# Edge sums of a graph layer: the node one-hot held still, the edge rows moved through it and accumulated by block

## The reference

```python
scores = jnp.einsum('ehd,ehd->eh', q[dst], k[src]) * scale      # 8 heads of 32
m = jax.ops.segment_max(scores, dst, num_segments=n)
ex = jnp.exp(scores - m[dst])
z = jax.ops.segment_sum(ex, dst, num_segments=n)
attn = ex / z[dst]
agg = jax.ops.segment_sum(attn[:, :, None] * v[src], dst, num_segments=n)
```

## Time and profile before

| | us |
|---|---|
| median of 3 runs | 5668.79 |
| the profiled execution, its span | 5667.8 |
| plan, clearing and first node pass | 0 to 576 |
| edge pass, layer 0 | 576 to 1972 |
| merge of ends | 1972 to 2117 |
| node pass "middle" | 2117 to 2905 |
| edge pass, layer 1 | 2907 to 4498 |
| merge of ends | 4498 to 4646 |
| node pass "last" | 4646 to 5560 |
| selection and store | 5560 to 5668 |

### The profile page before, as it was taken

The page is one execution under the profiler, slowest core; times in us unless marked ns, Lnnn a source line. Parts: engine busy times, 40 slices in busy tenths (PEclk is TensorE's granted clock), DMA queues, the critical chain, the costliest instruction groups (busy, mean ns, idle before and its releaser), DMA issues. The chain is left out here.

```text
span 5667.8 us, 110095 instructions
## 1 busy us (share of the span) xinstructions
PE 4558.0 (80%) x23706; PEld 3347.3 (59%) x23707; DVE 3879.3 (68%) x10653; ACT 1667.3 (29%) x5501; POOL 1786.4 (32%) x1733
## 2 busy tenths in 40 slices
PE   1666899999999857888878888888888658999993
PEld 1333566666666536666655555555555438888882
DVE  5888777777777756666666666666666746666665
ACT  0111233333333302222223222332332204444440
POOL 1000566666666400000035555555555300000000
PEclk9777999999999958999989998998998859999995
DMA  1111666666666401111135555555555310000001
GB/s 52 57 56 54 181 185 184 183 186 182 185 186 185 139 13 51 45 42 42 42 111 162 161 161 154 160 168 153 159 167 153 108 41 23 22 22 22 22 19 45
DMA packets 370226, 607.17 MB, mean 107 GB/s; under 512 B 136374, under 2 KB 221174, under 8 KB 370006
## 3 DMA queue, kind: packets, MB, share of 16 engines
q0 software_dynamic: 136960, 447.68, 27.1%
q1 hardware_dynamic: 233078, 157.70, 9.7%
HBM read 557.69 MB, written 48.27 MB: 107 GB/s over the span
## 5 line engine op out<-in xcount | busy, mean ns | idle before, releaser
L608 POOL DMA_INDIRECT edge_kv<-kv,edge_idx x1664 | 1742.0, 1047 | 2444.0 <-DMA edge_idx<-step_src 1248.1
L772 PE MATMUL edge_sums<-edge_sel,edge_kv 128*128 128x130 f32 x6656 | 1195.7, 304 | 126.4 <-DVE edge_kv L699 120.3
L815 ACT COPY acc<-edge_sums 128x384 f32 x1664 | 798.9, 480 | 1515.7 <-PE edge_sums L774 1478.8
L772 PEld LDWEIGHTS edge_sums<-edge_sel,edge_kv 128*128 128x128 f32 x6656 | 944.0, 198 | 448.8 <-issue 376.9
L734 PE MATMUL edge_q<-qc,edge_spread 128*128 x3328 | 939.7, 406 | 99.9 <-DVE edge_kv L650 76.1
L650 DVE TENSOR_TENSOR edge_kv<-edge_kv,edge_q 128x512 f32<-128x512 f32 x832 | 561.0, 674 | 447.7 <-DMA edge_kv<-kv,edge_idx 357.1
L734 PEld LDWEIGHTS edge_q<-qc,edge_spread 128*128 128x128 f32 x3328 | 583.4, 195 | 260.6 <-issue 213.5
L774 PE MATMUL edge_sums<-edge_sel,edge_wm 128*40 128x130 f32 x3328 | 713.7, 297 | 0.0
L699 DVE TENSOR_TENSOR edge_kv<-edge_kv,edge_wm 128x512 f32<-128x512 f32 x832 | 568.1, 683 | 113.5 <-ACT edge_wm L803 113.5
L657 DVE TENSOR_REDUCE edge_score<-edge_kv 128x16 f32<-128x512 f32 x832 | 557.8, 670 | 0.2
L774 PEld LDWEIGHTS edge_sums<-edge_sel,edge_wm 128*40 128x40 f32 x3328 | 256.8, 117 | 214.2 <-issue 22.6
(11 more groups left out here) (370 smaller groups left out, 5498.6 us busy)
## 6 DMA issues: line engine op xcount, KB each, us to landing
edge_rel<-step_rel SPq DMA_DIRECT2D x208, 256.0 KB
edge_kv<-kv,edge_idx POOLq DMA_INDIRECT x1664, 3.7
edge_flags<-step_flags SPq DMA_DIRECT2D x416, 32.0 KB
kv<-first_kv_out SPq DMA_DIRECT2D x49, 256.0 KB
kv<-middle_kv_out SPq DMA_DIRECT2D x49, 256.0 KB
h<-first_h SPq DMA_DIRECT2D x49, 128.0 KB
middle_h_in<-h SPq DMA_DIRECT2D x49, 128.0 KB
middle_v_in<-kv SPq DMA_DIRECT2D x49, 128.0 KB
```

The source lines that it names most:

```text
L608: nc.gpsimd.indirect_dma_start(kv[:, lane, j, :], None, dram["kv"], bass.IndirectOffsetOnAxis(ap=idx[:, turn[0], j:j + 1], axis=0)).then_i ...
L772: t.matmul(out[:, half * SELW:(half + 1) * SELW], kv[:, lane, j, D + half * P:D + (half + 1) * P], one_hot, start=True, stop=True)
L815: act_p.tick(s.copy(acc[:, :, bass.ds(at, P)], out[:, :, 0:P]), turn, f"acc{j}")
```

## The change

The product of a step is turned round. The one-hot of the node in its block (`sel`, now 128 columns, relative to the block and not to the step's first node) is the stationary side, and the edge's row of 272 columns (256 values, 8 weights, 8 maxima) is moved through it, so that sums arrive with nodes on the partitions. Steps of one block accumulate in one of four PSUM banks; a two-column matmul of zeros clears the accumulation state of the bank of the next block. ScalarE copies after every step the bank of the block before to `acc`, which now has 272 columns a block. The two end nodes are no columns of the one-hot any more: after each half of a group (four steps) four small matmuls with 2 stationary columns each write them at partitions 0, 32, 64 and 96 of a further bank, from where ScalarE copies them and SyncE stores them to memory. The gathers of steps 0 to 3 wait for `ends0`, of steps 4 to 7 for `ends1`. Register values are loaded for a pair at a time: two for q and four for the banks on TensorE, four on ScalarE. `qc` is now just q, `merge_ends` adds into `acc`, and neither is cleared.

```diff
-SELW = P + 2
-ZM = 40
+ROW = KV + 2 * H
+SUMS = 4
+BANKED = 512
+HALF = G // 2
...
+def values_of(nc, engine, ap, most):
+    engines = [e for e in mybir.ALL_ENGINES if e.name == engine]
+    assert len(engines) == 1
+    return nc.values_load_multi_w_load_instructions(ap, engines, min_val=0, max_val=most)[1]
...
-        kv = sb("kv", [P, 2, G, KV])
+        kv = sb("kv", [P, 2, G, ROW])
...
-        psa = [ps(f"sums{i}", [P, 512]) for i in range(ABUFS)]
+        psa = ps("sums", [P, SUMS * BANKED])
+        pse = ps("end_sums", [P, 512])
...
+            def store_ends(turn):
+                lane = turn[0]
+                act_p.wait(sp, turn, "ends1", beside=s_clear)
+                into = dram["erows"].rearrange("(b q w) n -> w b q n", q=HALF, w=2)
+                for q in range(HALF):
+                    sp.dma_start(into[:, bass.ds(number(later(turn, -1), 2), 4), q, :],
+                                 ends[32 * q:32 * q + 2, lane // 2, :, :]).then_inc(s_ends[lane // 2], 16)
...
                     if not first:
-                        pe_p.wait(pool, later(turn, -2), f"sums{j}", beside=s_clear)
+                        pe_p.wait(pool, later(turn, -2), f"ends{j // HALF}", beside=s_clear)
...
+            def sums_at(turn, m):
+                return values_of(nc, "PE", regs_s[0:1, turn[0], 4 * m:4 * m + 4], (SUMS - 1) * BANKED)
...
                 elif what == "tail":
+                    place = sums_at(turn, m)
                     dve_p.wait(pe, turn, f"value{m}")
                     for j in (2 * m, 2 * m + 1):
-                        if j >= ABUFS:
-                            act_p.wait(pe, turn, f"ends{j - ABUFS}")
+                        if j >= 2:
+                            act_p.wait(pe, turn, f"acc{j - 2}")
                         elif not earliest:
-                            act_p.wait(pe, later(turn, -1), f"ends{j + G - ABUFS}")
-                        one_hot = sel[:, j, :]
-                        out = psa[j % ABUFS]
-                        for half in range(2):
-                            t.matmul(out[:, half * SELW:(half + 1) * SELW],
-                                     kv[:, lane, j, D + half * P:D + (half + 1) * P], one_hot, start=True, stop=True)
-                        pe_p.tick(t.matmul(out[0:ZM, 2 * SELW:3 * SELW], wm[:, lane, j, :], one_hot,
-                                           start=True, stop=True), turn, f"sums{j}")
+                            act_p.wait(pe, later(turn, -1), f"acc{j + G - 2}")
+                        here, ahead = place[2 * (j % 2)], place[2 * (j % 2) + 1]
+                        t.matmul(psa[:, bass.ds(ahead, 2)], zeros[:, :], zeros[:, 0:2], start=True, stop=True,
+                                 skip_group_check=True)
+                        pe_p.tick(t.matmul(psa[:, bass.ds(here, QC)], sel[:, j, :], kv[:, lane, j, D:ROW],
+                                           start=False, stop=True, skip_group_check=True), turn, f"sums{j}")
+                    if m % 2 == 1:
+                        half = m // 2
+                        if half:
+                            act_p.wait(pe, turn, "ends0")
+                        elif not earliest:
+                            act_p.wait(pe, later(turn, -1), "ends1")
+                        for q in range(HALF):
+                            j = half * HALF + q
+                            mm = t.matmul(pse[32 * q:32 * q + 2, 0:QC], tab[:, turn[0], j, 2:4], kv[:, lane, j, D:ROW],
+                                          start=True, stop=True)
+                        pe_p.tick(mm, turn, f"ends{half}")
...
-                        out = psa[j % ABUFS][:, 0:3 * SELW].rearrange("p (c n) -> p c n", c=3)
-                        act_p.tick(s.copy(acc[:, :, bass.ds(at, P)], out[:, :, 0:P]), turn, f"acc{j}")
-                        act_p.tick(s.copy(ends[:, :, bass.ds(number(turn, 2 * G) + 2 * j, 2)], out[:, :, P:SELW]),
-                                   turn, f"ends{j}")
+                        act_p.tick(s.copy(acc[:, bass.ds(at, QC)], psa[:, bass.ds(bank, QC)]), turn, f"acc{j}")
+                    if m % 2 == 1:
+                        half = m // 2
+                        pe_p.wait(act, turn, f"ends{half}")
+                        if turn[0] % 2 == 0 and half == 0:
+                            room_for_ends(turn)
+                        act_p.tick(s.copy(ends[:, turn[0] // 2, 2 * lane + half, :], pse[:, 0:QC]),
+                                   turn, f"ends{half}")
```

In `plan_steps` six passes over 896 elements for the columns go, and the tables are written as one (`tab`: column, last, two end flags) with three register tables. In `merge_ends` the end rows are loaded from memory in three cuts, and 13 rounds of turning and scaling become three. In the node passes the stage `sums_t` (two transposes, a copy) and the addition of `qc` go:

```diff
-                elif stage == "sums_t":
-                    if exists(later(turn, -2)):
-                        pe_p.wait(act, later(turn, -2), "acc_t")
-                    act_p.tick(s.copy(ab[:, i, :, :], acc[:, 0:2, bass.ds(number(turn, P), P)]), turn, "acc")
...
-def clear_sums(nc, keep):
-
-    with nc.Block() as block:
-        @block.vector
-        def _(dve):
-            nc.vector.memset(keep["acc"][:, :, :], 0.0)
```

More of the change, by code:

```diff
@@ L185, in plan_steps @@
         col = sb("col", [P, SC, P])
[L186 removed]
+        both = sb("both", [P, SC, P])
         nf = sb("nf", [P, SC, P])
@@ L489, in edge_pass @@
         s_table = [sem(f"table{i}") for i in range(4)]
+        s_ends = [sem(f"ends{i}") for i in range(2)]
         s_row = [[sem(f"rows{i}_{j}") for j in range(G)] for i in range(2)]
@@ L501, in edge_pass @@
         dve_p.begin(dve_steps)
-        pe_p.begin([f"q{m}" for m in range(PAIRS)] + ["score_t", "max_t"] + [f"sums{j}" for j in range(G)])
-        act_p.begin(["weights"] + [f"{n}{j}" for j in range(G) for n in ("acc", "ends")])
+        pe_p.begin([f"q{m}" for m in range(PAIRS)] + ["score_t", "max_t"]
+                   + [f"sums{j}" for j in range(HALF)] + ["ends0"] + [f"sums{j}" for j in range(HALF, G)] + ["ends1"])
+        act_p.begin(["weights"] + [f"acc{j}" for j in range(HALF)] + ["ends0"]
+                    + [f"acc{j}" for j in range(HALF, G)] + ["ends1"])
         def fill(sems, depth, turn):
@@ L828, in _ @@
                 rest((3, None, GROUPS // 4 - 1), what, m, places)
+            act_p.wait(act, (3, None, GROUPS // 4 - 1), f"acc{G - 1}")
+            at = ((BLOCKS - 1) % SUMS) * BANKED
+            s.copy(acc[:, BLOCKS * QC:(BLOCKS + 1) * QC], psa[:, at:at + QC])
 LANES = 4
+CUTS = (0, 4, 8, ETILES)
 def merge_ends(nc, layer, dram, keep):
@@ L845, in sem @@
             return ctx.semaphore(f"merge{layer}_{name}")
-        ends, qc, ident = keep["ends"], keep["qc"], keep["ident"]
+        acc, ident = keep["acc"], keep["ident"]
         node = sb("node", [H, ENDS])
@@ L865, in merge_ends @@
         s_turned = sem("turned")
+        s_rows = [sem(f"rows{i}") for i in range(len(CUTS) - 1)]
         dve_p = Progress(nc, ctx, f"merge{layer}_dvep", LANES)
@@ L1063, in node_pass @@
         pt = [ps(f"pt{i}", [P, 512]) for i in range(2)]
-        sums = [ps(f"sums{i}", [P, 512]) for i in range(2)]
+        if kind == "last":
+            sums = [ps(f"sums{i}", [P, 512]) for i in range(2)]
         ph = [ps(f"ph{i}", [P, 1024]) for i in range(2)]
@@ L1498, in do @@
                     pe_p.tick(mm, turn, "qkv")
-                elif stage == "sums_t":
-                    act_p.wait(pe, turn, "acc", beside=s_weights)
-                    if exists(later(turn, -2)):
-                        dve_p.wait(pe, later(turn, -2), "agg", beside=s_weights)
-                    if kind == "last" and exists(later(turn, -4)):
-                        dve_p.wait(pe, later(turn, -4), "y_b", beside=s_weights)
-                    for half in range(2):
-                        mm = t.transpose(sums[i][:, half * P:(half + 1) * P], ab[:, i, half, :], ident[:, :])
-                    pe_p.tick(mm, turn, "acc_t")
                 elif stage == "turn_agg":
```

319 lines of the change are left out of this document (158 added, 161 removed).

## The result

| | before | after |
|---|---|---|
| median | 5669.43 us (4 runs, 5668.05 to 5679.23) | 6374.09 us (4 runs, 6367.51 to 6381.23) |
| profiled execution, span | 5667.8 | 6379.5 |
| edge pass, layer 0 | 1396.1 | 1868.4 |
| edge pass, layer 1 | 1591.0 | 1883.6 |
| all else | 2680.7 | 2627.5 |

The ratio is 1.123, 95% interval 1.121 to 1.125. The forecast was 6335 us, slower; it missed by 39 us. The edge passes grew by 472.3 and 292.6 us, all else lost 53.

What follows compares the result with a forecast made beforehand. The edge passes were taken as bound by a loop: gathers wait for TensorE's sums, VectorE for gathers. 5668.8 + 936 (longer period) - 195 (fetch stall) - 75 (elsewhere) = 6335 us; range 5620 to 6620, 8 in 10.

Steps and rivals of the forecast that it cites:

- Release and register loads: Edge passes: gathers 0 to 3 wait for a half's end sums, behind more register work; period up 4.5 us, +936 us.
- Loads of TensorE: TensorE's sequencer: register loads and checks grow from 1.4 to 2.6 us a pair, so step 2 starts at 8.7 us.
- rival 4: TensorE's sequencer: a load of four registers takes four times 0.3 us; 437 us more, 6772 us; chance 8%.
- The sums: TensorE, edge passes: a step's matmuls take 0.64 us instead of 0.98, so steps 2 and 3 take 1.3 us.
- The end sums: TensorE, end of a half: four small products take 1.7 us, between 0.5 side by side and 2.1 in a row.
- end sums under 1 us: Sign against the forecast: the four end products on TensorE taking less than 1 us together.
- Landing: Edge passes: gather 1's rows land 4.0 us after the gather starts, closing the period at 17.7 us.
- "The other half has slack": Edge passes: `ends1` comes some 6.7 us after `ends0`, its gathers needed 6 us after the next first product.
- Fetching: ScalarE's loop, second edge pass: its instruction-fetch stall most likely vanishes as the code moves, -195 us.
- Outside the edge passes: Clearing, merges, plan and node passes: dropped clears and two fewer transposes a block save 75 us in all.
- Rival 1: Edge passes: checks hidden and end sums side by side, period 14.0 us, 5565 us, faster than before; chance 15%.
- Rival 2: Edge passes: late release alone, checks hidden, end sums in a row; period 15.3 us, 5836 us; chance 22%.

Runs made afterwards that it cites:

- the release by pair: Kernel after with end sums issued two behind every two steps and each gather waiting only for those of its own pair: 6085.02 us.
- both together: Kernel after without range checks behind TensorE's register loads and with end sums and gather release pair by pair: 5523.23 us, ratio 0.973.
- the one-strip run: Kernel after with all four end products of a half written to the same output strip, one over the other: 6768.53 us.
- the shifted kernel: Kernel before with 48 already-satisfied waits on ScalarE ahead of the second edge pass's loop, moving its code: 5478.62 us, ratio 0.965.

## Why the prediction was right

| step, us after the first product | forecast | measured |
|---|---|---|
| product 1 ends | 3.4 | 3.2 |
| value product 1 ends | 6.1 | 6.0 |
| step 2 starts | 8.7 | 9.0 |
| step 3 ends | 10.0 | 11.2 |
| end sums end | 11.7 | 12.2 |
| gather 0 / gather 1 | 12.5 / 13.7 | 13.0 / 14.3 |
| period | 17.7 | 17.9, 18.0 |

The measured column is the median of 99 groups of the first pass; the last row holds both passes' means.

*Release and register loads* carry the result, and both are shown: 2.3 us by putting the release alone into before, 2.1 by taking the checks alone out of after, of 4.7. Going on from before, they add to 4.4. Some of the clock's cost is inside these numbers, since TensorE's granted clock fell with the release (1.00 to 0.92) and is 0.83 without the checks. Going back from after they don't: each remedy alone uncovers the other limit, as the release by pair and both together showed.

*Loads of TensorE.* The bank load takes 0.33 us for four values, as I took it (0.3); rival 4 (1.2) is out. The q load takes 0.54 for two, 0.24 more than I counted. Together step 2 is 0.3 late.

*The sums.* At the upper clock steps 2 and 3 take 1.3 us, clearing matmuls and all (the run with idle matmuls), as forecast. I had not predicted that the clock falls: as after ran they take 2.2, 0.9 more. This is the step that I missed, a consequence of the waits I had forecast: a TensorE that stands longer works slower afterwards (granted clock 1.00 in before, 0.92 with the late release alone, 0.81 in after), and here that was inside the chain.

*The end sums.* 1.7 forecast, 0.64 at the upper clock. I took a value near the upper end because no row showed two products beside each other. Standing side by side makes them cheaper than I took it: the one-strip run shows 2.00/0.64 = 3.1 for these four. The forecast's own list of signs had end sums under 1 us as one against it; the second half's took 0.64 and the first half's, at the lower clock, 1.08. The rule that I had set beside the 1.7 (Trainium skill, "TensorE: Matmul & The Clock Gate", Part 3) gives a factor of 2.38 for three strips, and by it, an estimate, 0.9 us. The trace agrees with it in kind, and for four strips it shows the 3.1. With 0.9 in place of 1.7 and nothing else changed, I would have forecast 166 us less and missed by more: this error and that of the clock offset each other. That the total came within 39 us is in part luck.

*Landing.* Gather 1 has landed after a median of 3.7 us and the product starts 0.12 later; 3.8 against 4.0. In before the same gather takes 4.4, in a pass where the DMA engines are busy 0.64 of the time and not 0.49.

*"The other half has slack"* is wrong. `ends1` ends at 17.7, 5.8 us behind `ends0`; the forecast said 6.7, though the terms it names add up to 6.3. Its gathers 4 to 7 issue one after the other, and gather 7, which the group's last product (product 3) needs, lands 0.12 us ahead of it. That product waits in 62 of 96 groups, for 0.4 us on the mean, and the count of 214 waits in 100 groups has these in it. The forecast's number survived because the two loops have nearly one length. I also missed TensorE's own order as a limit: with the release by pair, and the clock at 0.92, it stood at 16.55 us, right under the chain.

*Fetching.* Right: no stall in either pass, 197 us by the shifted kernel, 195 forecast. It explains that the second pass grew by 180 us less than the first. The rule named ahead of the forecast (Trainium skill, "Runtime: NRT & Kernel Launch", Instruction fetch mechanics) says that blocks hold 256 instructions and a window holds two. The trace agrees with it as far as it goes: ScalarE's loop is 286 instructions from branch to branch, a shift by 24 removes the stall and one by 256 restores it. By the rule such a loop lies in two blocks or touches three, depending on where it begins. Where the blocks begin, the trace does not show, so that the stalling loop touches three stays an inference.

*Outside the edge passes.* 75 us forecast, 53 measured: 18.5 up to the first edge pass (21 forecast), 20 for the merges (10 forecast), 14 for the two node passes (44 forecast). There TensorE's busy time fell by 18.4 and 18.7 us, just the two transposes a block, but the passes by 4.6 and 9.0: the transposes went beside work that other engines had to do anyway. That TensorE is busy 81% of a pass does not make each of its instructions part of the wait that ends last. Which wait it is there, no run tested.

*The sum.* 741 forecast for the edge passes, 765 measured. Rival 1, faster, is out at its own condition: steps 2 and 3 did not start early. Rival 2's period of 15.3 for the late release alone is near what the release in the kernel before gave (15.48) and what was left without checks (15.80): a fair price for a mechanism that was only half of the case.

## What to carry to other kernels

Where buffers are freed by one engine and refilled by another, a release that waits for more work lengthens every round by all that stands between, sequencer work included; look at what is queued ahead of the releasing instruction on its own engine, checks behind register loads too. Before taking one cost off a loop, add up the engine's whole order for a round: here each remedy alone won 430 and 289 us, and both 851, the clock's recovery with it. And before a loop with a constant share of "issue" in one place is redesigned, move its code by a few instructions.

## What the hardware showed that I had not expected

- ScalarE's loop of 286 instructions stalls once a round in one place of the program and not 24 instructions further: 197 us of 5670. Moved by 256, it stalls again.
- Four products of 2 stationary columns at four output strips take 0.64 us together, and 2.00 at one strip.
- One load of four bank values takes 0.33 us on TensorE's sequencer and one of two q values 0.54. Why the shorter one takes longer was not tried.
- Four idle matmuls a group raise the granted clock from 0.81 to 1.00 and save 195 us; the busy time of TensorE in 1000 us hardly grows (766.51 to 774.24 us).
